# One multiplication of the edge-count stage moved from VectorE to GpSimd in a graph-network kernel

## What is computed

```
edge_index = jnp.stack([src, dst])
x = _layernorm(x + _L0_gnn_ref(x, src, dst, deg_isqrt[:, None], node_vec1, ...), axis=-1)
x = _layernorm(x + _L1_gnn_ref(x, edge_index, ...), axis=-1)
x = _layernorm(x + _L2_gnn_ref(x, edge_index, ...), axis=-1)
x = _layernorm(x + _L3_gnn_ref(x, edge_index, edge_type_8, ...), axis=-1)
```

## Time and profile before

| | us |
|---|---|
| median of 3 executions | 5511.68 |
| lowest and highest of them | 5506.94, 5514.25 |
| the profiled execution, its own time | 5511.28 |
| span of its trace | 5509.6 |
| stage `count_edges`, first key to the end of the last copy | 61.2 to about 733 |

### The profile page before, as it was taken

The page is one execution under the profiler, slowest core; times in us unless marked ns, Lnnn a source line. Parts: engine busy times, 40 slices in busy tenths (PEclk is TensorE's granted clock), DMA queues, the critical chain, the costliest instruction groups (busy, mean ns, idle before and its releaser), DMA issues. The chain is left out here.

```text
span 5509.6 us, 107131 instructions
## 1 busy us (share of the span) xinstructions
PE 3854.9 (70%) x31278; PEld 2925.4 (53%) x31283; DVE 3861.6 (70%) x9964; ACT 2078.9 (38%) x2842; POOL 1418.6 (26%) x1703
## 2 busy tenths in 40 slices
PE   4666668743444554444545699998999879988997
PEld 2222248643444444444444455554555559986996
DVE  7999967656565556566563377774777778877887
ACT  2433334000111111111111256654556657765785
POOL 0000000006777777777777100000000000000000
PEclk8999989865555555555555699997999969997998
DMA  1111125532222222222212122211222121102111
GB/s 39 59 67 64 59 102 219 215 114 57 59 60 59 54 60 60 58 60 59 60 47 50 40 70 71 71 54 45 70 71 71 42 74 47 48 30 79 48 48 30
DMA packets 235224, 370.68 MB, mean 67 GB/s; under 512 B 169839, under 2 KB 175973, under 8 KB 235142
## 3 DMA queue, kind: packets, MB, share of 16 engines
q1 hardware_dynamic: 190006, 264.11, 14.8%
q0 software_dynamic: 41536, 85.08, 6.0%
q10 hardware_dynamic: 3600, 20.48, 0.9%
HBM read 292.58 MB, written 76.99 MB: 67 GB/s over the span
## 5 line engine op out<-in xcount | busy, mean ns | idle before, releaser
L1069 POOL DMA_INDIRECT en_got<-edge_q,en_now x1296 | 1306.1, 1008 | 409.2 <-issue 324.4
L1258 PE MATMUL en_t<-ident,en_got 128*128 128x128 f32 x1296 | 361.2, 434 | 959.4 <-DVE en_got L1152 959.4
L1296 ACT ACTIVATE en_hid<-en_t 128x512 f32<-128x512 f32 x324 | 193.5, 597 | 1651.0 <-DMA en_got<-edge_q,en_now 1409.4
L1258 PEld LDWEIGHTS en_t<-ident,en_got 128*128 128x128 f32 x1296 | 231.6, 217 | 1037.8 <-DVE en_got L1152 1037.8
L1266 PEld LDWEIGHTS en_o<-en_w2s,en_hid 128*128 128x128 f32 x2592 | 582.7, 333 | 0.0
L1266 PE MATMUL en_o<-en_w2s,en_hid 128*128 128x64 f32 x2592 | 577.4, 411 | 0.0
L1152 DVE TENSOR_TENSOR en_got<-en_got,p (+1 forms) x324 | 224.4, 693 | 496.3 <-ACTq L1290 463.6
L456 PE MATMUL cnt_ps<-cnt_hot_l,cnt_hot_k 128*128 128x400 bf16 x1600 | 360.2, 357 | 193.1 <-DVE cnt_hot_l L421 177.2
L1849 PE MATMUL r1s_ps<-hp,r1s_bits 128*128 128x193 bf16 x5000 | 423.1, 248 | 26.5 <-DVE r1s_bits L1802 13.6
L1849 PE MATMUL r0s_ps<-hp,r0s_bits 128*128 128x193 bf16 x5000 | 422.6, 247 | 26.5 <-DVE r0s_bits L1802 13.5
L1849 PEld LDWEIGHTS r1s_ps<-hp,r1s_bits 128*128 128x128 bf16 x5000 | 417.8, 98 | 31.8 <-issue 31.4
(11 more groups left out here) (389 smaller groups left out, 7399.8 us busy)
## 6 DMA issues: line engine op xcount, KB each, us to landing
en_got<-edge_q,en_now POOLq DMA_INDIRECT x1296
count_panels<-cnt_panel SPq DMA_DIRECT2D x25, 800.0 KB, 3.4
type_panels<-cnt_panel SPq DMA_DIRECT2D x25, 800.0 KB, 4.8
c0s_panel<-count_panels SPq DMA_DIRECT2D x25, 800.0 KB, 4.3
count_rows<-c0s_rows ACTq DMA_DIRECT2D x25, 800.0 KB, 3.5
c1s_panel<-count_panels SPq DMA_DIRECT2D x25, 800.0 KB, 6.0
c1s_rows<-count_rows SPq DMA_DIRECT2D x25, 800.0 KB, 7.5
en_raw<-count_panels SPq DMA_DIRECT2D x25, 800.0 KB
```

Of the source, the lines that this page charges most:

```text
L1069: pool.indirect_dma_start(out=got[:, i, j, :], out_offset=None, in_=k.q[:, :], in_offset=bass.IndirectOffsetOnAxis(ap=now[i][:, j:j + 1], ...
L1258: last = pe.transpose(tps[i % 2][:, j * P:(j + 1) * P], got[:, i, j, :], k.ident[:, :])
L1296: act.activation(hid[i % 2][:, :], tps[i % 2][:, :], ACT.Relu).then_inc(lined, 1)
```

## The change

VectorE no longer does L420 for the fixed tiles. GpSimd multiplies the plain keys of a step's two tiles by the edges' weights in one `tensor_tensor` of 128 x (2 x 128) and writes the weighed keys. A new semaphore `weighed` goes from GpSimd to TensorE, which waits for it in place of `hots`; GpSimd waits for `hots`. The more tiles stay as they were, all three instructions on VectorE.

```
+            with pool.Fori(0, WC - SETS + 1, SETS) as w:
+                for u in range(SETS):
+                    for s in range(STEPS):
+                        wait_alone(pool, hots, w * STEPS + (u * STEPS + s + 1), passed[2])
+                        pair = slice(2 * s, 2 * s + 2)
+                        pool.tensor_tensor(hot_k[:, u % 2, pair, 1, :], hot_k[:, u % 2, pair, 0, :],
+                                           now[u][:, pair, 2:3].broadcast_to([P, 2, P]), ALU.mult).then_inc(weighed, 1)
...
         @block.vector
...
             def fixed(w, u, s):
                 v.wait_ge(used, w * STEPS + (u * STEPS + s + 1))
                 for j in (2 * s, 2 * s + 1):
-                    last = tile([hot_k[:, u % 2, j, c, :] for c in range(2)], hot_l[:, u % 2, j, :], u,
-                                *(now[u][:, j, c:c + 1] for c in range(3)))
+                    v.tensor_scalar(hot_k[:, u % 2, j, 0, :], here[u][:, :], now[u][:, j, 1:2], None, ALU.is_equal)
+                    last = v.tensor_scalar(hot_l[:, u % 2, j, :], iota_l[:, :], now[u][:, j, 0:1], None, ALU.is_equal)
                 last.then_inc(hots, 1)
...
         @block.tensor
...
             def fixed(w, u, s):
-                pe.wait_ge(hots, w * STEPS + (u * STEPS + s + 1))
+                pe.wait_ge(weighed, w * STEPS + (u * STEPS + s + 1))
```

More of the change, by code:

```diff
@@ L379, in count_edges @@
         ps = [ctx.enter_context(nc.psum_tensor(f"cnt_ps{u}", [P, 2 * CUT], F32)) for u in range(SETS)]
-        iotas, own_v, ready, laid, hots, used, more_hots, more_used, copied, stored = map(
-            sem, ("iotas", "own", "ready", "laid", "hots", "used", "more_hots", "more_used", "copied", "stored"))
+        iotas, own_v, ready, laid, hots, weighed, used, more_hots, more_used, copied, stored = map(
+            sem, ("iotas", "own", "ready", "laid", "hots", "weighed", "used", "more_hots", "more_used", "copied", "stored"))
         passed = [sem(f"passed{e}") for e in range(3)]
```

## The result

| | before | after |
|---|---|---|
| median, us | 5506.9 (5 runs) | 5529.4 (5 runs, 5527.0 to 5533.8) |
| ratio to before, 95% interval | | 1.004 (1.0029 to 1.0051) |
| span of the trace | 5509.6 | 5532.0 |
| stage `count_edges`, first key to the end of the last copy | 671.6 | 687.5 |
| behind it, next stage's first matmul to the end | 4770.7 | 4777.9 |

The change costs 22 us, 0.4%. The forecast was 5525, some 14 us more. The stage grew by 15.9 us, and everything behind it by 7 in this one trace. Of the kernel before there is one trace. What the other 6 of the 22 us are stays open.

A forecast was written before the change was run, and what follows sets the result against it. VectorE was taken to bound the stage at 6.26 us a pair of windows; after the change, 2.80 + 2.75 + 0.90 + 0.30 + 0.1 = 6.85 against 6.71, so 5511 + 14 = 5525 us. Range 5452 to 5605, likeliest case 5500 to 5560.

The forecast's parts named there:

- L420's 176 us: VectorE work leaving the stage: 800 x 0.22 us, 1.76 a pair of windows, taken as the most it could lose.
- GpSimd's price, 0.70: Assumed duration in us of each of GpSimd's 400 weighing instructions, with 0.37 as low end and 1.56 as high end.
- the low estimate of two passes, 0.59: GpSimd's instruction priced as 0.37 us for one input plus 0.22 for a second input read in its own pass.
- Blocking, 0.55 an instruction: VectorE time lost waiting for each GpSimd instruction, in us; bounds 0 and 0.70; 4 x 0.55 a pair of windows.
- the ring: Even window's loop from VectorE through GpSimd, TensorE and ScalarE's copy and laying back to VectorE; 6.75 us a pair.
- The ring's ordinary turn: A pair without ScalarE's loop turn: even window 2.80 us, hand-over through TensorE and ScalarE 2.75, GpSimd's detour 0.90.
- the detour of 0.90: Longer way from VectorE to TensorE through GpSimd: 0.1 us semaphore, 0.1 half a VectorE instruction, 0.70 GpSimd's instruction.
- The turn of ScalarE's loop: Once in 8 windows ScalarE's `now` comes 1.2 us later, so 0.30 us a pair is added.
- the unplaced 0.10: Part of some 0.25 us a pair the prediction could not place, added to 6.75 to give 6.85.
- the break-even of 1.31 us: Blocking plus detour x at which the pair keeps its time: 2.25 + 2.75 + 0.40 + x = 6.71; forecast had 1.45.
- The mild rival: VectorE loses about 0.3 us per GpSimd instruction of 0.6: 21 us faster, 5490; without blocking 5437; chance 0.33.
- The whole-instruction rival: VectorE stands for GpSimd's whole instruction, 0.70 us: 69 us slower, 5580, or 5620 at 0.8; chance 0.15.

The follow-up runs named there:

- the early laying: Changed kernel, but ScalarE lays out windows w+2 and w+3 before copying window w; stage 627.6 us, kernel 5471.3, 0.994. Same in the kernel before: 654.4, 5487.1, 0.997.
- the floor: Changed kernel with the weighing left out, TensorE multiplying the plain keys twice, and late laying; stage 589.3 us, kernel 5429.7, 0.986 of before.

## Why the prediction was right, and where only by luck

The sign, the size (14 forecast, 22 measured, 16 in the stage) and the two mechanisms held. The single terms were off by up to 0.14 us, as much as the forecast effect on a pair, and cancel in part. From every start to start of VectorE in the stage's traces (669 and 685 us from its first to its last), against 0.16, 0.22 and 0.23 us:

| us in the stage | before | after |
|---|---|---|
| VectorE's own starts | 635 | 458 |
| held up by GpSimd | 0 (none of its instructions) | 128.5 (316 times, 0.41 each) |
| standing for ScalarE, TensorE or loads | 34 | 98 |

- *L420's 176 us*: right as VectorE's work. That the stage could lose at most that was an idle bound: with the weighing left out it loses 82.
- *GpSimd's price, 0.70*: 0.61 where it meets nobody, 0.65 in the mean, a little under the 0.7 to 0.9 named for the profile. Right in kind; the low estimate of two passes, 0.59, was the better one.
- *Blocking, 0.55 an instruction*: over-sized. It is 0.41 in the mean (mostly 0.36 to 0.46), and 88 of the 400 hold up nobody. This was the largest term for VectorE: 4 x 0.55 would be 220 us in the stage, and it is 128.5. In the ring, by which the forecast goes, only the even window's part counts, and that was nearly right: an even window takes 2.77 in the mean (2.30 of VectorE's own work and 0.47 held up, 114 times in 100 windows) where I had 2.80. The reading that the blocking was taken from was itself off, to the low side: three casts of the same size with no ramp beside them take 0.54 each (15.50 to 17.11 in the trace before; int32 to f32, the other way round), so the cast beside the ramp will have lost about 0.30 and not 0.22, as the one that I compared it with had a ramp beside it too.
- *The ring's ordinary turn*: the detour of 0.90 was 0.83 (from VectorE's last L434 to TensorE 1.24, where it was 0.41). Left out was the 0.13 from the end of `here` to VectorE's start, so the ring had 0.22 us to spare before, and not 0.35. The pair shown above took 6.26 where I had 6.45; over all pairs without a turn of ScalarE's loop the mean is 6.54.
- *The turn of ScalarE's loop*: right in the mean. I added 1.2 us once in four pairs; the 25 pairs with a turn take 7.79 in the mean, 1.25 more than the others. Single ones are worse: the one from 361.34 to 369.55 took 8.21, as its even window also held a second blocking and the copy started late. Its last rows:

```profile
366.64 0.90 ACT L512 ACTIVATE cnt_panel<-cnt_ps 128x400 f32 x2 [2.56 <-PE cnt_ps L463]
...
368.91 0.21 ACT L501 ACTIVATE cnt_now<-cnt_keys 128x12 f32 x1 [1.38 <-issue]
...
369.55 0.26 DVE L433 TENSOR_SCALAR cnt_hot_k<-cnt_here,cnt_now 128x128 bf16<-128x128 int16 x1 [1.97 <-ACT cnt_here L502]
```

Per pair 6.85 was forecast and 6.88 is 687.5 / 100. That the ring sets the pace was right, and is shown by the early laying; that the sum came out within 0.03 was luck in part. For VectorE as a whole blocking was taken too large (2.20 a pair, measured 1.28) and standing too small (6.85 - 6.70, some 15 us in the stage, measured 98). In the ring the detour was 0.07 too long, the even window 0.03 too long, the 0.13 to VectorE's start was missing, and the unplaced 0.10 stood for the rest. How thin this is shows in the break-even of 1.31 us for blocking plus detour: with the measured 0.41 and 0.83 it is 1.24, which would have made the change 7 us faster. What made it slower are the terms that this formula lacks: 0.06 more of blocking in an even window (0.47), 0.05 more of VectorE's own work there (2.30 for 2.25), and the 0.13. With them it is 1.48, 17 us slower, and 16 were measured.

Of what the profile after should show: VectorE's idle time before a window grew from 31.3 to 94 us and `here` ends it in 90 of 100 pairs, as named. The stage of 685 was 687.5. Wrong was that L421 would be lengthened above all. On the fixed tiles it is not longer at all (L434 has 316 ns, 331 before), and L419 little (L433 has 294, 262 before). Most lengthened is the more tiles' L427 (558 ns), since GpSimd starts about 0.2 us behind the end of the first step's last instruction (404.20 and 404.38 in the pair above), and in windows with more tiles that is where VectorE is then.

The mild rival (faster) failed on the ring, not on the blocking: its blocking of 0.3 is nearer to the measured 0.41 than mine. With the ring cut it comes true, 27 us faster for GpSimd's part. The whole-instruction rival had the mechanism right, since VectorE comes back when GpSimd's instruction ends. Its sum was too large: the instruction is 0.61 to 0.75 and not 0.70 to 0.80, 0.15 to 0.33 of it costs nothing, and part falls where VectorE stands anyway.

## What to carry to other kernels

When work moves to an engine that holds up the first one, compare what the first engine loses by each instruction, which is its whole duration less 0.15 to 0.33 us here, with what the first engine is relieved of in the same step: here 0.41 for 0.44, next to nothing. Look then at which hand-over gets longer: a stage bound by an engine had a second ring 0.22 us behind it, and 0.83 us of detour made that the bound. Moving one call ahead of another (the early laying) was worth 60 us to the changed kernel, nearly four times what the change cost the stage (16 us), and splitting the work over two helpers was the fastest version tried.

## What the runs showed of the hardware

- A `tensor_tensor` of GpSimd with two inputs took 0.61 us for 256 and 1.04 for 512 elements where it did not wait for VectorE: 1.68 ns an element and 0.18 fixed, worked out from these two.
- VectorE stands until GpSimd's instruction ends, though the two share no data: its next start lies within 0.05 us of that end, for 256 and for 512 elements. It loses the instruction's duration less 0.15 to 0.33 us. GpSimd waits for VectorE's instruction under way, at most 0.14 us here (0.61 to 0.75).
- GpSimd's chained semaphore counts, which touch no memory, hold up nobody: VectorE lost under 0.5 us beside 15 of them a step (0.08 us from one to the next).
- ScalarE's activations on the same tiles hold up nobody: VectorE's means were 249 and 318 ns beside 800 of them, 249 and 317 with none.
- A load of loop bounds into VectorE's registers, which shows as 1.3 us in all in the stage before, shows as up to 2.0 us of standing at a time where VectorE has less queued work (32 us in 22 places of the floor).
- The same gather stage took 1806 to 1808 us in two traces of one kernel and 1789 to 1798 in all others, its code unchanged. What makes the difference is open.
